# Expert stage of a two-layer ViT tower: half of the gates spread by DMA, units in pairs, one product in eight on GpSimd

## The reference, cut

```python
z = jnp.einsum('nd,sdr->nsr', xf, P)            # 8 segments of 16
scores = jnp.einsum('nsr,smr->nsm', z, C)       # 64 experts per segment
topv, topi = jax.lax.top_k(scores, K)           # K = 4
w = jax.nn.softmax(topv, axis=-1)
...
h = jax.nn.gelu(jnp.einsum('nsr,nskrh->nskh', z, W1g) + b1g)   # 32 hidden
yl = jnp.einsum('nskh,nskhr->nskr', h, W2g) + b2g
comb = jnp.einsum('nskr,nsk->nsr', yl, w)
out = jax.nn.gelu(comb @ G1 + g1b) @ G2 + g2b
```

## Time and profile before

| | us |
|---|---|
| three runs | 952.45, 959.13, 961.68 |
| median | 959.13 |
| the profiled execution | 950.38 |
| its span (first to last instruction) | 948.3 |
| expert units, first to last product | 634.5 to 921.9 |
| mean granted PE clock over the span | 0.851 |

### The profile page before, as it was taken

One profiled execution on the slowest core, in us unless ns is written; L12 is line 12 of the kernel. 1 busy time (PEld: TensorE's weight loads), 2 busy tenths in 40 slices (PEclk: granted clock), 3 DMA queues, 4 the chain that ended last, 5 costly groups with the idle time before them and its releaser, 6 DMA issues.

```text
span 948.3 us, 17188 instructions
## 1 busy us (share of the span) xinstructions
PE 768.0 (81%) x6440; PEld 425.4 (45%) x6440; DVE 539.9 (57%) x1499; ACT 381.0 (40%) x786; POOL 149.0 (16%) x187
## 2 busy tenths in 40 slices
PE   5989997797877785558889897448888988899992
PEld 3667766653333333236666666223333333333331
DVE  5666567401110111158685867737877686878776
ACT  0432424132111110023443343236777676768760
POOL 0030321322221000040111010322202122200002
PEclk9977779579798686669998999758888998999997
DMA  7611000049999999690000000570002000200001
GB/s 300 255 39 38 4 1 2 1 169 423 425 424 414 410 422 363 108 110 4 2 2 0 0 1 2 158 97 1 1 1 51 1 1 1 51 5 2 1 1 39
DMA packets 25017, 102.66 MB, mean 108 GB/s; under 512 B 3551, under 2 KB 14755, under 8 KB 20723
## 3 DMA queue, kind: packets, MB, share of 16 engines
q1 hardware_dynamic: 23894, 98.36, 31.0%
q0 software_dynamic: 1056, 3.44, 0.9%
HBM read 93.08 MB, written 5.07 MB: 103 GB/s over the span
## 4 chain that ended last, share of the span: by engine, by line
PE 58%; DVE 17%; DMA 13%; issue 4%; ACT 2%; POOL 2%; SPq 1%; DVEq 0%; POOLq 0%; ACTq 0%
DMA stream<-in_fc_dram 13%; PE P L1670 9%; PE P L1638 8%; PE P L1648 8%; PE P L367 6%; PE P L795 3%; PE P L439 3%; PE P L410 3%; PE P L1132 2%; PE P L423 2%; DVE work L603 2%; DVE work L504 1%; DVE early L483 1%; PE P L1663 1%; PE P L764 1%
## 5 line engine op out<-in xcount | busy, mean ns | idle before, releaser
L1895 DVE TENSOR_TENSOR work<-work,P 128x384 f32<-128x384 f32 (+1 forms) x384 | 197.5, 560 | 73.5 <-PE P L1648 60.5
L1777 ACT ACTIVATE work<-P 128x384 f32<-128x384 f32 (+1 forms) x384 | 177.7, 500 | 71.5 <-PE P L1638 63.5
L1638 PE MATMUL P<-stream 99*128 99x384 bf16 (+1 forms) x384 | 136.1, 355 | 20.4 <-ACT work L1777 13.4
L1648 PE MATMUL P<-early,middle 96*128 96x384 bf16 (+1 forms) x384 | 135.5, 353 | 11.0 <-DVE work L1895 5.8
L1638 PEld LDWEIGHTS P<-stream 99*128 99x128 bf16 x384 | 38.9, 102 | 119.6 <-ACT work L1777 67.6
L1670 PE MATMUL P<-work 128*32 128x384 f32 (+1 forms) x768 | 89.7, 539 | 0.0
L822 ACT ACTIVATE work<-P 128x768 f32<-128x768 f32 x16 | 13.0, 811 | 157.2 <-PE P L777 157.2
L514 ACT ACTIVATE work<-work 101x444 f32<-101x444 f32 x48 | 28.1, 585 | 103.9 <-DVE work L509 103.9
L837 DVE COPY work<-P 128x768 f32<-128x768 f32 x16 | 15.3, 958 | 94.8 <-PE P L785 94.8
L1648 PEld LDWEIGHTS P<-early,middle 96*128 96x128 bf16 x384 | 39.2, 102 | 50.0 <-DVE work L1895 27.7
L608 POOL TENSOR_SCALAR work<-work 101x4 f32<-101x4 f32 x12 | 2.8, 229 | 345.1 <-DVE work L598 345.1
(11 more groups left out here) (254 smaller groups left out, 1261.6 us busy)
## 6 DMA issues: line engine op xcount, KB each, us to landing
stream<-in_fc_dram SPq DMA_DIRECT2D x16, 2304.0 KB
stream<-in_fc_dram SPq DMA_DIRECT2D x16, 1536.0 KB, 18.3
stream<-in_fc_dram SPq DMA_DIRECT2D x16, 768.0 KB, 19.7
early<-in_patches_dram SPq DMA_DIRECT2D x4, 888.0 KB, 5.1
stream<-w_dram SPq DMA_DIRECT2D x6, 512.0 KB
early<-stream SPq DMA_DIRECT2D x24, 96.0 KB, 3.1
work<-in_w_dram SPq DMA_DIRECT2D x1, 2048.0 KB, 7.7
stream<-z_dram SPq DMA_DIRECT2D x6, 297.0 KB, 10.2
```

The source lines that it names most:

```text
L1638: pe.matmul(P[:, n % 3, 0:WIDE[c]], w1s[:, seg, (hh * (CH // 2) + i) * 128:(hh * (CH // 2) + i + 1) * 128], zs[:, seg, part_of(c)], start= ...
L1648: pe.matmul(P[:, 3 + n % 3, 0:WIDE[c]], gate_sel[:, i, :], ws[:, 2 * (4 * sq + j) + hh, part_of(c)], start=True, stop=True).then_inc(s_bc, 1)
L1777: act.activation(act_out[:, n % 4, 0:cols], P[:, n % 3, 0:cols], ACT.Gelu_apprx_tanh).then_inc(s_ua, 1)
L1895: dve.tensor_tensor(gated[:, n % 8, 0:cols], act_out[:, n % 4, 0:cols], P[:, 3 + n % 3, 0:cols], ALU.mult).then_inc(s_ug, 1)
```

## The change

1. Units go in pairs: ACT and DVE handle two units (j = 0, 1 or j = 2, 3) with one instruction of 128 x 2 x 384 (or 416). `GROUP` lists 96 groups of four units; pair p = 2g + x. PSUM banks 0 to 3 hold hidden pairs, 4 and 5 one gate pair.
2. Pair x = 0 gets its gates by PE as before (`gate_pair`). Pair x = 1 gets them from `gate_rest`, an fp32 copy that SP stores to `gate_dram` and loads back, each row on 32 partitions, into a ring of four buffers (`load_spread`, 96 DMAs). `gate_parts` and its staging keep only the x = 0 half; 12 DMAs of 32 x 2 x 384 per chunk.
3. Every eighth pair (p % 8 == 7, 24 of 192) is multiplied by POOL.
4. `last_bias`: 6 bf16 matmuls and one fp32, in place of 12 bf16.
5. In `moe_pe` the first matrix of group 15 comes ahead of the second of group 14.
6. The splitting of W1, b1, b2, gate_sel goes from the slot mixture to layer 1's quads 0 to 2, with its DMAs on SP (`split_sync`); the MEMSET of `zs` goes from layer 1's start to quad 3. Some buffers are placed elsewhere, and a few semaphores are merged.

The core of the diff (b2_rest, the buffers' places and the pairs' forms of the selection steps left out):

```diff
+        gate_dram = [dram(f"gate_dram{c}", [2, SM, 2, cols], f32) for c, cols in enumerate((384, 384, 416))]
...
+            first(GROUPS // 2 - 1, 1)
             second(GROUPS // 2 - 1, 0)
-            first(GROUPS // 2 - 1, 1)
             second(GROUPS // 2 - 1, 1)
...
+                if it < 2:
+                    split_w1(pool, 2 * it)
+                    split_w1(pool, 2 * it + 1)
+                elif it == 2:
+                    split_w1(pool, 4)
+                    split_b2(pool)
+                elif it == 3:
+
+                    pool.wait_ge(s_split_out, 16 * 5)
+                    pool.wait_ge(s_h3, it)
+                    pool.memset(zs[6 * SR:ZR, :, :], 1.0).then_inc(s_set, 1)
+                    pool.wait_ge(s_set, 1)
...
+        def split(pool, base, src, out):
+            pool.tensor_copy(out[:, 0, :], src).then_inc(s_split, 1)
+            pool.wait_ge(s_split, base + 1)
+            pool.tensor_tensor(src, src, out[:, 0, :], ALU.subtract).then_inc(s_split, 1)
+            pool.wait_ge(s_split, base + 2)
+            pool.tensor_copy(out[:, 1, :], src).then_inc(s_split, 1)
+            pool.wait_ge(s_split, base + 3)
+            pool.tensor_tensor(out[:, 2, :], src, out[:, 1, :], ALU.subtract).then_inc(s_split, 1)
...
+            def load_spread(g):
+
+                c, sq, hh, i = GROUP[g]
+                if g % NG == 0:
+                    sp.wait_ge(s_gd, 32 * (1, 4, 8)[c])
+                if g >= RING:
+                    product_made(sp, 2 * (g - RING) + 1)
+                row = 32 * hh + 4 * i
+                src = gate_dram[c][sq, row:row + 4].rearrange("r k t -> r (k t)")
+                sp.dma_start(spread_gates(g).rearrange("p k t -> p (k t)"), spread(src, 1, 32)).then_inc(s_sg[g % RING], 16)
+
+            store_gates(0, 2)
+            stage_chunk(0)
+            for g in range(3 * NG):
+                for t in range(FIRST, TT):
+                    if g == (BEGINS[t] + 16) // 2 + RING + 1:
+                        store_gates(t, t)
+                if g in (NG, 2 * NG):
+                    stage_chunk(g // NG)
+                load_spread(g)
...
+            def hidden_pair(g, x):
+                c, sq, hh, i = GROUP[g]
+                if g:
+
+                    pe.wait_ge(s_ua, 2 * (g - 1) + x + 1)
+                for j in (2 * x, 2 * x + 1):
+                    seg = 4 * sq + j
+                    mm = pe.matmul(P[:, j, 0:WIDE[c]], w1s[:, seg, (hh * (CH // 2) + i) * 128:(hh * (CH // 2) + i + 1) * 128],
+                                   zs[:, seg, part_of(c)], start=True, stop=True)
+                mm.then_inc(s_u1, 1)
...
+            for g in range(3 * NG):
+                if g + 1 < 3 * NG:
+                    hidden_pair(g + 1, 0)
+                if g:
+                    expert_out(g - 1)
+                if g + 1 < 3 * NG:
+                    hidden_pair(g + 1, 1)
+                    gate_pair(g + 1)
...
+                if not on_pool(p):
+                    dve.wait_ge(s_ua, p + 1)
+                    if x:
+                        dve.wait_ge(s_sg[g % RING], 16 * (g // RING + 1))
+                        by = spread_gates(g)
+                    else:
+                        dve.wait_ge(s_bc, g + 1)
+                        by = P[:, 4:6, 0:cols]
```

More of the change, by code:

```diff
@@ L45 @@
 LOW = -3.0e38
-WORK = 12400
+WORK = 12560
 def tower(nc, io):
@@ L1042, in l1_pool @@
             pool_rstd(pool, L0, QUADS)
-            pool.wait_ge(s_fo, GROUPS)
-            pool.wait_ge(L0["rstd"], QUADS + 1)
-            pool.memset(zs[6 * SR:ZR, :, :], 1.0).then_inc(s_set, 1)
-            pool.wait_ge(s_set, 1)
-            steps(pool, step)
+            for it in range(QUADS):
+                step(it, it == 0, it + 1 == QUADS)
         def prep_pe(pe):
@@ L1578, in mlp_sync, with store_gates @@
                 sp.dma_start(zs[SR * k:SR * (k + 1), :, :], zv[part]).then_inc(s_zs, 16)
-            for n in range(3):
+            def store_gates(first, last):
+                sp.wait_ge(s_gr, last + 1)
+                c = first // 3 if first < 9 else 2
+                here = slice(128 * first, min(128 * (last + 1), FROM[c] + WIDE[c]))
+                for k in range(2):
+                    dst = gate_dram[c].rearrange("q r k t -> k r q t")[k]
+                    sp.dma_start(dst[:, :, here.start - FROM[c]:here.stop - FROM[c]],
+                                 gate_rest[SM * k:SM * (k + 1), :, here]).then_inc(s_gd, 16)
@@ L1959, in mlp_pool, with product @@
                 third_part(t)
-            for t in range(FIRST, TT):
-                shifted_scores(t)
-                scaled(t)
-                parts(t)
+            def product(p):
+                g = p // 2
+                pool.wait_ge(s_ua, p + 1)
+                pool.wait_ge(s_sg[g % RING], 16 * (g // RING + 1))
+                if g >= 2:
+                    pool.wait_ge(s_u2, g - 1)
+                at = 4 * (g % 2) + 2
+                pool.tensor_tensor(gated[:, at:at + 2, 0:WIDE[g // NG]], act_out[p % 4][:, :, 0:WIDE[g // NG]],
+                                   spread_gates(g), ALU.mult).then_inc(s_up, 1)
+            last = (s_g2, FIRST)
+            for p in range(6 * NG):
+                for step, at, made in ((shifted_scores, 4, s_sh), (scaled, 10, s_gn), (parts, 16, s_g2)):
+                    t = beside(p, at)
+                    if t:
+                        pool.wait_ge(*last)
+                        step(t)
+                        last = (made, t + 1)
+                if on_pool(p):
+                    pool.wait_ge(*last)
+                    product(p)
+                    last = (s_up, p // 8 + 1)
         summed, normed = (attn, xn), (h_out, h_in)
@@ L2027, in _ @@
             moe_sync(sp)
+            split_sync(sp)
             mlp_sync(sp)
```

328 lines of the change are left out of this document (169 added, 159 removed).

## The result

| | before | after |
|---|---|---|
| median, us | 955.79 (4 runs) | 1052.64 (4 runs, 1049.43 to 1056.25) |
| span of the profiled execution | 948.3 | 1051.6 |
| first product of the units, us | 634.5 | 624.3 |
| last product begins, us | 921.3 | 1020.8 |

The change makes the kernel slower: the ratio is 1.1009, 95% interval 1.093 to 1.1088. The forecast was 1043.

A forecast was written before the change was run, and what follows sets the result against it. TensorE's order of work was taken to bound the expert stage, with spread copies to replace it as the bound. 950.4 + 105 (copies) - 7.6 (mixture's end) - 5 (splits and MEMSET) = 1042.8, stated as 1043 us, range 1000 to 1082.

The forecast's parts named there:

- The spread copies: Expert stage: gate copies through DRAM are slower than the work they feed and set the pace, +105 us.
- four engines per copy: Expert stage: four of 16 DMA engines serve each spread copy at 25.7 GB/s each, 3.83 or 4.15 us per copy.
- The sum: Whole kernel: profiled execution plus all terms, 950.4 + 105 - 7.6 - 5 = 1042.8 us.
- Rival A: Expert stage: all 16 engines serve each copy, hidden at 0.96 us; total 900 us (885 to 912), chance 0.10.
- B: Expert stage: 16 engines per copy, but GpSimd products hold VectorE, 36 us; total 936 us, chance 0.06.
- Rival C: Expert stage: four engines, each slower than 25.7 GB/s; at 20 GB/s about 1125 us in all, chance 0.13.
- D: Whole kernel: gains and copies cancel at 2.9 us per copy, time within 1%, chance 0.03.
- The mixture's end: Slot mixture's end: doing group 15's first matrix ahead of a weight wait gains 7.6 us (6 to 11).
- The splits and the MEMSET: Second layer: moving the MEMSET to quad 3 and W1's split into quads 0 to 2, -5 us (0 to -8).
- Products on GpSimd: Expert stage: 24 of 192 pair products on GpSimd, about 1.74 us each, nothing on the path.
- a share above 0.4: Expert stage: sign that would prove the prediction wrong; the DMA share was expected near 0.25.
- under 60% of the stage: Expert stage: expected sign, TensorE busy for less than this part and partly at its lower clock.

The follow-up runs named there:

- k16: Changed kernel with hidden units re-laid so each spread copy's source has slowest dimension 32, not 4, same bytes: 903.91 us, 0.9491 of the kernel before.
- k8: Changed kernel with each spread copy reading eight rows 16 times instead of four rows 32 times, same bytes: 930.92 us in one run.
- before_moe: Kernel before with only group 15's first matrix put ahead of group 14's second at the slot mixture's end: 951.39 us, ratio 0.9946.
- before_both: Kernel before with both the new matrix order at the slot mixture's end and the MEMSET of zs moved to quad 3: 946.60 us, ratio 0.9875.
- before_memset: Kernel before with only the MEMSET of zs moved from the second layer's start to its quad 3: 946.62 us, ratio 0.9871.
- k16_nopool: k16 with all 192 pair products on VectorE, none on GpSimd: 901.68 us, 0.9472 of the kernel before.

## Why the prediction was right, and where a step was not

**The spread copies.** The step that decided, four engines per copy at 25.7 GB/s, held: 102 to 103 GB/s at a share of 0.26 to 0.28, 25.5 to 25.8 each, and groups 4.19 us apart in the third chunk where 4.15 was the price. The sum had 388 us from the first landing (638) to the last product (1026), for 95 copies; measured are 629.1 to 1020.8, 391.7 us. That is 4.12 us per copy with everything that goes in between, against 4.08. Rivals A and B asked for 16 engines, and k16 shows what they would have brought: 903.91 us, where A said 900 and B 936. C (fewer bytes per second and engine) and D didn't come with four engines. Rival A's "from seven engines on" took 25.7 GB/s for each, though, and with eight engines k8 has about 17 to 19 each and isn't hidden.

The Trainium skill, page "DMA: Bandwidth & Descriptors", section "Why a DMA increments its semaphore by 16 and not by 1", gives the rule of the slowest dimension and of the lowest-numbered engines. The runs agree with the first: shares of 0.14, 0.28 and 0.50 for slowest dimensions of 2, 4 and 8. That a second queue gained nothing agrees with the engines being the same for both queues; which numbers they have, no trace here shows.

**The mixture's end.** -7.6 was forecast and -7.0 came, but the step "the new order does these 8.2 us ahead of that wait" was wrong: the order alone moved the end by 0.06 us in before_moe, and in before_both not at all to the good. What I passed over is that the wait for group 15's own second matrix ("late next: the copy for group 15") was due at the same time, 385.28 us, since the whole stage runs at the pace of its stream (share 1.01 in the earlier trace rows). I had the split's 3.44 MB in the diff and never priced them: at 411 GB/s they are 8.4 us. The number was right by luck.

**The splits and the MEMSET.** -5 was taken between 0 and -8. At the place the start of the second layer gained: VectorE's four scalings take 3.05 us, where they took 9.38 and in before_memset take 1.44, so the split's first steps, which now run there, give 1.6 back. Behind that, the attention from its first projection to the load of w2 takes 185.4 us, against 181.6 before. The windows of this stretch, of before, after, before_memset, before_moe and k8 (whose code up to there is the changed kernel's), with the granted clock in the third place from the end:

```profile
415.67:597.31 181.64, 157.66 (x1777) 117.15 (x1778) 130.83 (x379) 70.10 (x150) 17.02 (x20) 0.93 0.06 8
```

```profile
402.13:587.57 185.44, 162.37 (x1777) 120.70 (x1778) 131.41 (x379) 70.02 (x150) 40.15 (x43) 0.90 0.19 32
```

```profile
408.49:594.70 186.21, 163.31 (x1777) 120.96 (x1778) 131.05 (x379) 70.10 (x150) 25.07 (x21) 0.90 0.10 12
```

```profile
415.69:608.50 192.81, 172.09 (x1777) 127.24 (x1778) 131.70 (x379) 70.02 (x150) 17.03 (x20) 0.85 0.06 7
```

```profile
402.13:597.15 195.02, 174.11 (x1777) 128.07 (x1778) 131.91 (x379) 70.02 (x150) 40.14 (x43) 0.84 0.18 30
```

The lengths go with the clock: 181.6 us at 0.93, 185.4 and 186.2 at 0.90, 192.8 at 0.85, 195.0 at 0.84. At 0.90 the changed kernel with the splits is no slower than before_memset without them, so the 3.8 us can't be put down to the splits; they fit the lower clock, though no run sets the clock by itself, and why one execution is granted less than another stays open. Together the units began 10.2 us earlier, where I had 12.6; 7.0 of it are the mixture's, which leaves 3.2 for the 5 of this term.

**The rest.** The sum was 1042.8 and the profiled execution took 1053.64 us, 10.8 more. The last product begins at 1020.8, 7.4 us later than 1026 - 12.6: half because the first copy's product came at 629.1 and not at 625.4, half in the copies. The first copy was issued at 622.0, 2 us later than the sum had it, and its product came 7.1 us behind that, where the sum had 1.5 + 3.83; the 1.5 us "to begin" was an assumption that no row shows. The other 3.8 us lie behind the start of the last product, 32.8 us against 29.1: it is one of GpSimd's (1.94 us against 0.59 on VectorE before), and the tail behind it takes 1051.6 - 1022.8 = 28.8 us against 26.4.

Four figures of the prediction don't add up as written. 1012.1 and 12 make 1024, not 1026, so the sum should be 1041. At 27 GB/s the copies end at 993.4 and not at 995.4. Rival C at 20 GB/s per engine comes to about 1147 by its own copies of 4.9 and 5.3 us, not 1125. Two pairs of 2 x 0.58 us make 2.3 us and not 2.1 (measured: 0.97 + 1.01). None of them turns the forecast.

**Products on GpSimd.** They cost nothing that k16 against k16_nopool can tell; beside four-row copies no run tried it. The 1.74 us estimated from 1157 ns for 512 columns came out at 1.80 to 1.99. They do stand in the chain, 1.95 us of each 16.74, but only as what the next copy waits for while the engines still have three copies queued. That a GpSimd product "stops VectorE's work on SBUF operands" is not shown: beside a GpSimd product at 849.01 to 850.99 us of k16 stands a VectorE product that reads PSUM, and it keeps its 1.02 us; for products with both operands in SBUF no run isolates it.

**What would have shown me wrong** was a share above 0.4; it was 0.28. One sign failed: I said TensorE would be busy for under 60% of the stage, and it was 280.37 of 382 us, 73%, since expert_out has 155.5 us of busy time in place of 89.7. Without these 66 us it is 56%.

## What to carry to other kernels

Before a DMA that repeats rows is put in place of compute, look at the slowest dimension of both its sides: four rows read 32 times each used four engines here, and the same bytes as 32 repeats of four rows used all sixteen. That one swap of dimensions, with the weights permuted to suit, turned this change from 10% slower to 5% faster. A second queue didn't help where the engines were the limit; nor should more buffers, by the same argument, though no run tried them. And when a stage runs at the pace of a stream, price every byte that shares the stage before believing in a new order of work, and look at the place in the trace before believing a difference of medians.

## What was not expected of the hardware

- The rate of an engine isn't the same for each form of these copies. With two and four engines it was 53 / 2 = 26.5 and 103 / 4 = 25.8 GB/s over the stage. With eight (k8) the share was 0.50, eight engines' worth, at 151 GB/s, or 18.9 GB/s each. In k16 it was 413 / 16 = 25.8 GB/s in the half microsecond shown, but 163 GB/s at a mean share of 0.52, or 19.6 for each busy engine, over the stage; a copy of 384 KB took 3.4 us from issue to landing, where I had expected about one, and four buffers hid it. Why, no run here tells. The row of the page of k16 (KB each, median us to landing):

```profile
early<-gate_dram SPq DMA_DIRECT2D x64, 384.0 KB, 3.4
```

- GpSimd's MEMSET of 8.01 us held a VectorE TENSOR_SCALAR from SBUF to SBUF for its whole length, but nothing that read PSUM, and neither a RECIPROCAL nor a TENSOR_TENSOR with SBUF operands alone. The Trainium skill, page "SBUF — State Buffer", section "Who interferes with whom", calls the shared port pair an exclusive lock; the trace agrees, with 8.23 us for a scaling that else takes about 0.36.
- Eight halves of expert_out took 0.91 us together, and four alone 0.89: taking the products by pairs raises TensorE's busy time (155.5 against 89.7 us), and would cost time where TensorE doesn't wait anyway. In k16, where both pairs' products are there in time, all eight run in 0.91 us again.
